# A two-layer attention and expert kernel on one core: the routing weights' reciprocal as a 321st column of a token's row, ScalarE's first tanh earlier, repeated products on TensorE, side work three experts later, and two pairs of layer 2 on VectorE

## What is computed

```
xn = layernorm(x)
s  = attention_0(xn)        # 16 heads that share one key and one value of 128
f  = experts(xn) + shared_mlp(xn)      # 64 experts, 8 of them for a token
x  = x + s * silu(f)
xn = layernorm(x)
s  = attention_1(xn)        # sequence of 2 (the batch), 16 heads of 16, causal
f  = bitlinear(gelu(bitlinear(xn, w_fc)), w_proj)     # ternary weights
x  = x + s * silu(f)

route: scores = sigmoid(xn @ router.T); sc = scores + e_bias
       4 of 8 groups by the sum of their two best sc, then the 8 best sc
       w = scores[chosen] / (sum of the chosen scores + 1e-20) * 2.5
expert e: (silu(xg @ gate) * (xg @ up)) @ down * w, at most 128 tokens each
```

## Time and profile before

| what | value |
|---|---|
| time, median of 3 runs | 415.77 us (414.70 to 416.57) |
| the profiled execution: its time, its span | 417.58 us, 415.6 us |
| PE busy | 335.9 us (81%) |
| DVE busy | 287.7 us (69%) |
| POOL busy | 227.1 us (55%) |
| ACT busy | 206.6 us (50%) |
| chain that ended last | PE 37%, DVE 17%, issue 15%, DMA 11%, POOL 10%, ACT 9% |

### The profile page before, as it was taken

How to read it: one execution, slowest core, us unless ns; L and a number is a source line. 1 busy time by engine, 2 the same in 40 slices (tenths; PEclk the granted TensorE clock), 3 DMA queues, 4 the chain that set the end, 5 groups by cost and what they waited for, 6 DMA issues and landing times.

```text
span 415.6 us, 7026 instructions
## 1 busy us (share of the span) xinstructions
PE 335.9 (81%) x2091; PEld 268.4 (65%) x2091; DVE 287.7 (69%) x946; ACT 206.6 (50%) x548; POOL 227.1 (55%) x212
## 2 busy tenths in 40 slices
PE   3979598789997997779989889694079888988893
PEld 3764277567786784668867778483057767877772
DVE  5799843787776654236755357844559988899875
ACT  2575954434244343264443234421057778666781
POOL 6000034566878774678788888765165544663311
PEclk9999876999999999889999889979569999999999
DMA  7976165758787897967887768445930000000001
GB/s 251 372 218 238 28 187 170 196 125 183 153 194 151 214 256 211 284 146 142 204 199 175 155 144 198 87 62 67 299 96 0 27 1 28 27 25 28 3 25 50
DMA packets 37943, 58.39 MB, mean 140 GB/s; under 512 B 6203, under 2 KB 27283, under 8 KB 37523
## 3 DMA queue, kind: packets, MB, share of 16 engines
...
q0 software_dynamic: 12288, 18.88, 25.2%
...
## 4 chain that ended last, share of the span: by engine, by line
PE 37%; DVE 17%; issue 15%; DMA 11%; POOL 10%; ACT 9%; POOLq 0%; DVEq 0%; ACTq 0%
DMA acc_d<-W,idxE 8%; PE ps L1526 6%; PE ps L1574 5%; POOL acc_d L517 4%; PE ps L1586 4%; PE ps L1488 3%; PE ps L1396 3%; DVE F L1292 3%; PE ps L1425 3%; DMA W<-tok_d,idxE 2%; POOL ny L556 2%; POOL W L495 2%; PE ps L1563 2%; ACT ps L834 2%; ACT W L847 2%
## 5 line engine op out<-in xcount | busy, mean ns | idle before, releaser
L517 POOL DMA_INDIRECT acc_d<-W,idxE x64 | 101.8, 1590 | 44.2 <-DVE W L1126 24.1
L495 POOL DMA_INDIRECT W<-tok_d,idxE x56 | 57.0, 1017 | 62.8 <-DVE idxE L1097 46.0
L1162 DVE SCALAR_TENSOR_TENSOR W<-W,ps 128x88 f32<-128x88 f32 x64 | 15.5, 242 | 65.9 <-ACT W L777 58.3
L761 ACT ACTIVATE W<-ps 128x256 f32<-128x256 f32 x64 | 24.4, 381 | 47.4 <-PE ps L1563 41.1
L1526 PE MATMUL ps<-A,v 128*128 128x128 f32 x256 | 37.7, 309 | 9.1 <-issue 9.1
L1526 PEld LDWEIGHTS ps<-A,v 128*128 128x128 f32 x256 | 36.0, 222 | 12.0 <-issue 11.4
L1704 PE MATMUL ps<-W,A 128*128 128x257 f16 x256 | 30.0, 273 | 10.3 <-DVE F L1317 9.6
L1671 PE MATMUL ps<-F,wfcT 128*128 128x256 f16 x256 | 32.6, 282 | 3.0 <-DVE F L1255 3.0
L1126 DVE TENSOR_SCALAR W<-ps,W 128x256 f32<-128x256 f32 x56 | 26.8, 479 | 11.5 <-PE ps L1586 6.8
L1704 PEld LDWEIGHTS ps<-W,A 128*128 128x128 f16 x256 | 24.0, 98 | 15.9 <-DVE F L1317 11.4
L834 ACT ACTIVATE ps<-ps,gwv 128x512 f32<-128x512 f32 x32 | 21.4, 667 | 24.4 <-PE ps L1671 24.4
...
## 6 DMA issues: line engine op xcount, KB each, us to landing
...
```

Source lines behind the costliest of these rows:

```text
L495: pool.indirect_dma_start(out=xg[n % XR], out_offset=None, in_=tok_d[:, :], in_offset=bass.IndirectOffsetOnAxis(ap=idxE[:, n:n + 1], axis=0))\
L517: pool.indirect_dma_start(out=acc_d[SIDE[n]][:, :], out_offset=bass.IndirectOffsetOnAxis(ap=idxE[:, n:n + 1], axis=0), in_=ysb[n % YS], in ...
L761: sc.activation(xgT[n % 2], bk_(2)[:, 0:D].rearrange("p (k n) -> p k n", k=KH), ACT.Copy)\
```

## The change

- A token's row in DRAM has 321 numbers instead of 320 (`ROW`); the last is the reciprocal of its sum of scores, times 1.25. `weights` is gone; the scores are stored as they are, and `put` multiplies by both columns, where it had the second factor 0.5 as a constant. Buffers in SBUF are moved to make room.
- ScalarE does `logit_tanh(0)` after `take_x(7)`, and `root(4)` behind it and behind `normal(8)` and `normal(9)`. TensorE does `router_shared(7)` ahead of the transpose of tile 8. VectorE does the reciprocal of the last four tiles in the middle of `choose_groups(0)`. Tiles 10 and 11 are normalised on POOL.
- TensorE does 12 products of the identity with itself at the start (`WARM0`) and 10 of 512 columns ahead of layer 2 (`WARM1`); nobody reads them.
- `positions(1)` stands ahead of `keys(3)`; `turn_v(1)` behind `shared_turn(1)`; ScalarE's and VectorE's programs follow.
- `START` is 7 instead of 4, and the shared MLP's second half and the sums of `Wo` begin 1 and 4 experts later.
- Pair 1 of layer 2 goes through VectorE as pair 0 did; POOL begins with pair 2.

```diff
-START = 4
+START = 7
-BY_DVE = (10, 11)
+LATE = 4
+WARM0, WARM1 = 12, 10
+BY_POOL = (10, 11)
-SH_TURN, SH_DOWN = {0: 2, 1: 3}, {1: 2, 2: 3}
-WOS_AT = (2, 3, 4, 5)
+ROW, XS = D + NE + 1, 328
+SH_TURN, SH_DOWN = {1: 2, 2: 3}, {2: 2, 3: 3}
+WOS_AT = (6, 7, 8, 9)
...
-    tok_d = nc.dram_tensor("tok_d", (NTOK + P, D + NE), F32, kind="Internal").ap()
+    tok_d = nc.dram_tensor("tok_d", (NTOK + P, ROW), F32, kind="Internal").ap()
...
+            for t in BY_POOL:
+                pool.wait_ge(nmr_ready, 1)
+                pool.tensor_scalar(xn[:, t, :], x[:, t, :], mv[:, t, 0:1], rstd[:, t:t + 1], ALU.subtract, ALU.mult)\
+                    .then_inc(xn_pool, 1)
...
-            def weights(f):
-
-                sc.wait_ge(rden_ready, f + 1)
-                for t in range(HT * f, HT * f + HT):
-                    ins = sc.activation(s_w[:, t, :], s_w[:, t, :], ACT.Copy, scale=rden[:, t:t + 1])
-                ins.then_inc(w_ready, 1)
...
             take_x(7)
+            logit_tanh(0)
             normal(8)
             normal(9)
+            root(4)
             take_x(8)
-            root(4)
-            logit_tanh(0)
...
             take_keys(0)
+            weight_sums(0)
             shared_gate(1)
-            weight_sums(0)
             take_keys(1)
             take_keys(2)
-            weights(0)
+            weight_sums(1)
             take_keys(3)
-            weight_sums(1)
+            number(0)
             take_v(0)
-            number(0)
-            weights(1)
-            take_v(1)
...
                 then(ve.tensor_tensor(t_lo1, sc_g[:, :, 0:4], sc_g[:, :, 4:8], ALU.min))
+                if f == 0:
+                    inverse(LATE)
+                    minus_mean(LATE)
...
-                then(ve.tensor_scalar(den[:, cols], den[:, cols], 2e-20, 1.0 / ROUTE_SCALE, ALU.add, ALU.mult))
-                ve.reciprocal(rden[:, cols], den[:, cols]).then_inc(rden_ready, 1)
+                then(ve.tensor_scalar(den[:, cols], den[:, cols], 2e-20, 2.0 / ROUTE_SCALE, ALU.add, ALU.mult))
+                ve.reciprocal(half(s_w, f)[:, :, NE], den[:, cols]).then_inc(w_ready, 1)
...
-                ve.tensor_scalar(ysb[n % YS], bk_(3)[:, 0:D], xg[n % XR][:, D + n:D + n + 1], 0.5, ALU.mult, ALU.mult)\
+                ve.tensor_scalar(ysb[n % YS], bk_(3)[:, 0:D], xg[n % XR][:, D + n:D + n + 1], xg[n % XR][:, D + NE:ROW],
+                                 ALU.mult, ALU.mult)\
...
             take_projected(NT - 1)
             centre_weights()
-            first_total()
-            for p in range(-AHEAD, NP):
+            first_total(0)
+            silu(0)
+            first_add(0)
+            for p in range(-2, NP):
                 if 0 <= p + 1 < NP:
                     low_x(p + 1)
+                if p == -1:
+                    silu(1)
+                    first_add(1)
...
+                if p == -2:
+                    first_total(1)
...
             pe.wait_ge(ident_ready, 1)
+            for _ in range(WARM0):
+                pe.matmul(bk_(7)[:, 0:P], ident[:, :], ident[:, :], start=True, stop=True)
...
             for t in range(NT):
+                if t == HT:
+                    router_shared(t - 1)
...
             keys(2)
+            positions(1)
             keys(3)
-            positions(1)
             turn_v(0)
-            turn_v(1)
...
             shared_turn(1)
+            turn_v(1)
             indices(0)
...
             pe.wait_ge(wpj2_ready, 1)
+            pe.wait_ge(acc_ready, 1)
+            for _ in range(WARM1):
+                pe.matmul(bk_(7), ones16[:, :], wfcT[:, 0, 0:512], start=True, stop=True)
```

103 lines of the change are left out of this document (54 added, 49 removed).

## The result

| | before | changed kernel |
|---|---|---|
| median over the runs of the comparison | 415.16 us (412.87 to 419.08, 20 runs) | 412.75 us (408.80 to 417.17, 20 runs) |
| ratio of the times, 95% interval | | 0.9941 (0.9917 to 0.9964) |
| a second comparison | 415.97 us (23 runs) | 413.83 us (12 runs), 0.9969 (0.9936 to 1.0001) |
| the profiled execution: its time, its span | 417.58, 415.6 us | 411.87, 410.0 us |

The change brings 2.4 us, where 6.6 us were forecast; the time lies inside the range. The second comparison has 2.1 us, and its interval just reaches no change. One execution of either kernel differs from the next by several microseconds, so the two spans, 5.6 us apart, say too much.

A forecast was written before the change was run, and what follows sets the result against it. It took chains of waits as the bound: engine relays in stage 1 and layer 2's start, slow first experts, then POOL's gathers and scatters. Terms of 3.1 + 2.0 + 1.5 = 6.6 us gave a median of 409.2 us, range 404 to 415.5.

The forecast's parts named there:

- term 1: Stage 1 to the first expert: 3.1 us less, with the first list 1.7 us sooner.
- term 2: First experts of stage 2, up to scatter 7: 2.0 us less, 37.8 instead of 39.8 us.
- term 3: Layer 2: 1.5 us less, with ends of 0 and 2.5 us.
- I take it to hold: Before `slots(0)`: TensorE's clock stays up through 2.2 us of idleness, so `slots(0)` takes 1.9 us.
- I follow this relay tile by tile: Stage 1: ScalarE's last copies at 32.5 us, `keys(0)` 1.9 us later, VectorE's gain shrunk to 0.1 us.
- So scatter 0 comes 7.8 us after the start instead of 10.8: Stage 2's start: scatter 0 sooner because `shared_turn(3)` and `shared_down(2)` now stand behind `down(0)`.
- I take that wait for the store's: Scatter 2: its 1.07 us wait is for the shared MLP's last store, so it comes 21.8 us after the start.
- The rival (0.12): Scatter 2 waits for its row's named DMA, not the store, coming 5.5 us sooner: 403.7 us; chance 0.12.
- Attention then packs 64 steps into 57 experts. I price that at nothing.: Stage 2: packing into 57 experts instead of 60 costs nothing, TensorE being busy 6.45 of 8 us.
- TensorE becomes the bound of stage 2: Stage 2: 3.9 us of attention moves to where TensorE has 1.5 of 8 us left: 413.1 us; chance 0.12.
- The slower rival: Gathers and scatters: the 1284-byte row starts off 256-byte multiples, costing up to 11.8 us: 421.0 us; chance 0.07.
- The clock falls again: Before `slots(0)` and in layer 2: term 1 shrinks to 0.9, term 3 to 0.7: 412.2 us; chance 0.17.

The follow-up runs named there:

- a_warm2: Changed kernel with 7 more repeated products of the identity between `turn_v(0)` and `slots(0)`; ratio to before 0.9888.
- a_tanhlate: Changed kernel with ScalarE's first tanh behind `root(4)` again, as before; ratio to before 0.9888.
- best1: Changed kernel with ScalarE's first tanh where it was before and 7 repeated products between `turn_v(0)` and `slots(0)`; 411.4 us, ratio to before 0.9899.
- best1b: Second comparison of the changed kernel with the late tanh and 7 repeated products before `slots(0)`; 411.0 us, ratio to before 0.9880.
- combo3: Changed kernel with late tanh, 7 repeated products before `slots(0)`, 16 instead of 10 ahead of `turn_x(0)` and 6 behind it; 411.7 us, ratio 0.9915.
- before2: The kernel before, unchanged, run and profiled once more; ratio to before 0.9985.
- b_l2: Kernel before with pair 1 of layer 2 on VectorE alone, no repeated products, nothing else of the change; ratio to before 0.9994.
- a_start4: Changed kernel with `START` 4, the shared MLP's side work and the sums of `Wo` at the experts of before; ratio to before 0.9982.
- after2: The changed kernel, unchanged, run and profiled once more; ratio to before 0.9969.
- b_start: Kernel before with `START` 7, the shared MLP's second half and sums of `Wo` one and four experts later; 413.55 us, ratio to before 0.9967.

## Why the prediction came out too large

**Where the time is missing.** From the first piece of `x` to the first turn of stage 2 the changed kernel has 58.0 and 59.3 us, the kernel before 59.4 and 58.5: between 0.8 lost and 1.4 won, where term 1 had 3.1. From there to the last scatter it is 221.5 and 220.9 us, against 223.6, 223.7 and 220.7 in the three profiles of the old order: at most 2.8 won, where term 2 had 2.0. Layer 2 won 1.6 to 1.9 us, where term 3 had 1.5. So most of the shortfall is term 1's; term 2 came out near its size by errors that offset each other, which is luck.

**Term 1, the list: forecast 1.7 us, measured a loss of 0.3 to 2.3 from the first piece of `x` on.** Two steps failed.

- "I take it to hold." The clock fell in the wait of 2.0 us before `slots(0)`. By that `slots(0)` took 2.96 and 2.95 us instead of 1.9 and the turns 1.7 instead of 0.9: 1.9 us. The stretch at 80 to 82 us, which I took as the nearer one, was no measure of it, and the fall in 48 to 52 us was; that rival had 0.17. `a_warm2` proves it, with 1.5 us back.
- "I follow this relay tile by tile." Its last copies ended at 32.06 us, 21.6 after the third root, where I had 20.9 and before had 18.5 (its third root is at 12.18 us, ahead of the reciprocal in the earlier trace rows); den's sum came 28.05 us after that root, where I had 27.0 and before 26.55. The early tanh loses 1.0 us on the path (`a_tanhlate`); that it does so because the copies of tiles 8 and 9 and with them `keys(0)` stand behind two table loads is read from their order and not tested by itself. I had added both effects up and found them even. Its risk for the clock I had not seen at all.

With both mended (`best1`, `best1b`, `combo3`) the gather is issued 44.7 us after the third root, and the forecast had 44.5 (56.1 - 11.6): nothing else in this term was far off. Its last addition is loose, though: 1.7 us at `slots(0)` and 0.8 at the turn less 0.45 are 2.0, not 1.7. The 1.7 it states is what `a_warm2` has, 4.2 us from the start of `slots(0)` to the gather instead of 5.9.

Right in it was the sooner root, about half a microsecond where I had 0.6, if executions with the same normalisation at 8 us are compared: 6.8 to 7.1 us from the first piece to the third root against 7.5 in `before2` where it took 0.73 us, and 7.5 to 7.7 against 7.9 to 8.1 where it took 1.45 to 1.47. Right was VectorE's wait of a microsecond (1.00), too. **The Trainium skill**, "ScalarE: Activation LUTs", section "What ACT_TABLE_LOAD costs", has 1.38 us of drain on top of each load. Both loads here end 0.02 us before the next operation (15.40 + 1.28 and 16.70; 18.29 + 1.28 and 19.59), so the trace disagrees again.

**Term 1, the first expert: forecast 1.4 us, measured 1.5 to 1.6.** From the gather to the first turn 4.1 us instead of 5.7 and 5.6. The size is right by luck: the shared MLP's copy still ends the wait, where I had said the landing would.

**Term 2: forecast 2.0 us up to scatter 7, measured 3 to 6, and then 2 to 3 given back.** From the first turn I had 7.8 us to scatter 0, 5.3 to scatter 1, 8.7 to scatter 2 and 16.0 to scatter 7. The first profile after has 10.0, 5.6, 3.2 and 16.0, together 34.8 instead of 37.8. The last step, POOL's pace without attention, is right. Three others failed:

- "So scatter 0 comes 7.8 us after the start instead of 10.8." The 10.8 us were not the side work. TensorE's clock was at 0.50 in 64 to 68 us of that execution, and so in `b_l2` (10.8 us too); in `before2`, with the same order and a clock of 1.00 there, scatter 0 comes after 7.8 us. The changed kernel has 10.0 and 8.4. No run shows a gain here, and what makes it 8.4 or 10.0 is open.
- "I take that wait for the store's." The wait of 1.07 us in the earlier trace rows was neither the store's nor that of the DMA which the row names: scatter 2 is the first on its accumulator and waits for no scatter. It waited for VectorE's `put(2)`, which ended at 83.23 us, 0.28 us ahead of it, in all three profiles of the old order, just as `put(0)` ends 0.28 us ahead of scatter 0. And `put(2)` stood behind attention's first step: VectorE's maximum, ScalarE's exponential after it, and only then the expert's own work:

```profile
79.42 1.21 DVE L1018 TENSOR_REDUCE nmax<-ps 128x1 f32<-128x1024 f32 x1
80.66 1.11 ACT L738 ACTIVATE A<-ps,nmax 128x1024 f32<-128x1024 f32 x1 [4.38 <-DVE nmax L1018]
82.31 0.24 DVE L1162 SCALAR_TENSOR_TENSOR W<-W,ps 128x88 f32<-128x88 f32 x1 [1.68 <-ACT W L777]
82.75 0.48 DVE L1126 TENSOR_SCALAR W<-ps,W 128x256 f32<-128x256 f32 x1
```

`a_start4` has this again (`put(2)` ends at 82.25 us, scatter 2 follows at 82.53). With attention later the store does end the wait in ten of thirteen profiles, by 0.9 to 1.7 us, but 4.0 to 4.8 us after ScalarE's last copy, and not the 7.85 us (75.66 to 83.51) that I had carried over. `after2`:

```profile
81.02 1.58 POOL L526 DMA_INDIRECT acc_d<-W,idxE  x1 [0.89 <-DMA acc_d<-xn]
```

So the cost of the store was the mis-sized term. The rival (0.12) had the 3.2 us from scatter 1 to scatter 2 in the first profile, but the wrong releaser, and a time, 403.7 us, that no run of this change came near.

- "Attention then packs 64 steps into 57 experts. I price that at nothing." From scatter 7 to scatter 9 it takes 8.6 and 9.7 us after and 8.5 in `b_start`, against 6.4 to 6.5 in the three profiles of the old order. (From scatter 9 to the last one it is 178.2 and 177.7 us, against 177.5, 179.8 and 175.9: no difference that can be told.) The windows I read, at 120 to 128 us, lie behind the place that decides. At experts 7 to 9 VectorE has the moved sums of `Wo` (4 x 1.21 us), the second list and attention's first tiles at once; the prediction named the move of `WOS_AT` nowhere and said of VectorE that it wasn't the bound. The rival "TensorE becomes the bound of stage 2" had the place nearly, but the wrong engine: TensorE waits for VectorE there, and only then does its own clock add to it.

**Term 3: forecast 1.5 us, measured 1.6 to 1.9.** Right in size, by a different path: pair 1 on VectorE gives 1.2 us, and `WARM1` 0.4. "The first eight of them take 0.95 us" failed: the clock had fallen again within 1.5 us. So the first gelu is 2.0 us sooner after the first sum, not 2.5. With that mended (`combo3`) the gelu is 0.8 us sooner still and the end is not, as the ends of 0 and 2.5 us had allowed.

**The row.** The slower rival (0.07) is excluded: 105.0 and 105.3 us of queue, POOL's period still 3.19 us. The Trainium skill, "DMA: Bandwidth & Descriptors", section "How a descriptor splits into AXI transactions", says that the bytes ahead of an unaligned start are fetched too, unused, and still cost beats. No run here shows such a cost in the queue's busy time.

**The rivals' times.** "The clock falls again" had the right mechanism, before `slots(0)` and in layer 2, and 412.2 us is near the measured 412.75. That it is so near is luck in part: it had neither the early tanh's loss nor what term 2 won and gave back. The same goes for the TensorE rival's 413.1.

**Sum.** In the two kernels' first profiles: stage 1 +0.3 us, first turn -1.6, to scatter 7 -5.0, to the last scatter +2.9, layer 2 -1.8, and `x` on the chip 0.3 sooner, together -5.6 as the spans say. The second profiles of the two are 3.3 us apart, the medians 2.4. Part of the difference is known: before's first profile had a slow start of stage 2 (45.4 us to scatter 7; 43.1 and 44.0 in the other two of that code), and the changed kernel's a good stage 1 (54.0 us; 55.2 in the second). My sum was made against one execution, and 3.0 us of its scatter 0 rest on that slow start.
